# Message phase of a four-layer graph network: the offset adds go from GpSimd to VectorE, the ring of gathered rows gets seven tiles, and the one-hot of types moves to the end of VectorE's turn

## The reference, cut to what matters

```
x = layernorm(x + L0(x));  x = layernorm(x + L1(x));  ...

def L1(x):                       # 12500 edges, 16 edge types
    m_in = concat([x[src], edge_emb_W[edge_type]])
    m    = relu(m_in @ msg_W.T + msg_b)
    agg  = segment_sum(m, dst) / clip(degree, 1)
    h    = x + agg @ upd_W.T + upd_b
    return (h - mean) * rsqrt(var + 1e-5) * ln_g + ln_b
```

## Time and profile before

| | us |
|---|---|
| median of three runs | 2611.82 |
| the profiled execution's own time | 2617.21 |
| its span, first to last instruction | 2615.3 |
| DVE busy in the span | 1591.5 (61%) |
| POOL busy in the span | 1868.5 (71%) |
| PE busy in the span | 1428.1 (55%) |
| first scan (L1538) of the message phase starts | 727.97 |
| last scan starts | 1106.39 |
| first gather of the message phase starts | 702.67 |

### The profile page before, as it was taken

One profiled execution on the slowest core, in us unless ns is written; L12 is line 12 of the kernel. 1 busy time (PEld: TensorE's weight loads), 2 busy tenths in 40 slices (PEclk: granted clock), 3 DMA queues, 4 the chain that ended last, 5 costly groups with the idle time before them and its releaser, 6 DMA issues. The chain is left out here.

```text
span 2615.3 us, 21930 instructions
## 1 busy us (share of the span) xinstructions
PE 1428.1 (55%) x4580; PEld 736.3 (28%) x4580; DVE 1591.5 (61%) x4851; ACT 863.5 (33%) x1813; POOL 1868.5 (71%) x1494
## 2 busy tenths in 40 slices
PE   6787588887356665637787547445445650011111
PEld 1344244444222222213333224222222330011110
DVE  8889287777438888948777735234334565434443
ACT  0111167676326565644566612111112330000000
POOL 5773777876288887334677777777875877777787
PEclk8899699998577778769888878777777875555555
DMA  1111344433434554334454466666696883333331
GB/s 25 26 35 33 96 116 129 129 109 76 106 75 115 133 128 129 98 93 104 105 120 116 105 151 186 176 170 168 187 165 205 224 220 96 82 68 71 76 70 43
DMA packets 358129, 297.95 MB, mean 114 GB/s; under 512 B 110941, under 2 KB 312428, under 8 KB 357981
## 3 DMA queue, kind: packets, MB, share of 16 engines
q1 hardware_dynamic: 260397, 225.43, 31.5%
q0 software_dynamic: 97600, 71.11, 13.9%
HBM read 199.75 MB, written 96.70 MB: 113 GB/s over the span
## 5 line engine op out<-in xcount | busy, mean ns | idle before, releaser
L2089 PE MATMUL tl_pX<-k_ident,tl_ga 125*128 125x125 f32 x400 | 84.1, 348 | 427.9 <-DMA tl_ga<-table_TE,k_s_idxE 327.1
L2200 DVE TENSOR_TENSOR_SCAN tl_S<-tl_same,tl_S,tl_pX 128x500 f32<-128x500 bf16 x96 | 120.3, 1253 | 312.9 <-issue 181.8
L479 POOL DMA_INDIRECT tl_ga<-table_TE,k_s_idxE x200 | 242.9, 1215 | 63.4 <-issue 59.1
L2089 PEld LDWEIGHTS tl_pX<-k_ident,tl_ga 125*128 125x128 f32 x400 | 58.1, 178 | 442.4 <-DMA tl_ga<-table_TE,k_s_idxE 336.7
L479 POOL DMA_INDIRECT eq_ga<-table_T,k_idxS x100 | 124.5, 1245 | 80.8 <-ACT eq_y L1794 51.7
L479 POOL DMA_INDIRECT ms_ga<-table_T,k_idxS x100 | 134.3, 1343 | 50.8 <-issue 41.0
L479 POOL DMA_INDIRECT at_ga<-x,k_src x100 | 138.4, 1384 | 43.4 <-issue 25.2
L1269 PE MATMUL tl_pCon<-dr_BC,dn_cT 128*128 128x512 f32 x196 | 133.1, 768 | 51.8 <-ACT dn_cT L1276 25.5
L479 POOL DMA_INDIRECT tl_ga<-table_TH,k_send x100 | 123.0, 1230 | 51.2 <-issue 50.6
L281 POOL DMA_INDIRECT table_ptab<-k_ef,ix_scatI x100 | 124.9, 1249 | 46.4 <-issue 46.4
L479 POOL DMA_INDIRECT at_gb<-xw,at_dstI x100 | 129.8, 1298 | 30.5 <-issue 30.5
(11 more groups left out here) (464 smaller groups left out, 4445.9 us busy)
## 6 DMA issues: line engine op xcount, KB each, us to landing
dr_x<-x SPq DMA_DIRECT2D x97, 256.0 KB
result<-dr_o SPq DMA_DIRECT2D x97, 256.0 KB
dm_xT<-xT SPq DMA_DIRECT2D x32, 768.0 KB
tl_fac<-table_dinv SPq DMA_DIRECT2D x50, 250.0 KB
table_T<-at_y SPq DMA_DIRECT2D x50, 224.0 KB
table_T<-ms_y SPq DMA_DIRECT2D x50, 224.0 KB
table_T<-eq_y SPq DMA_DIRECT2D x50, 224.0 KB
table_TE<-tl_y SPq DMA_DIRECT2D x50, 224.0 KB
```

What stands on the lines that cost most here:

```text
L479: nc.gpsimd.indirect_dma_start(out=buf[:, k, :], out_offset=None, in_=table, in_offset=bass.IndirectOffsetOnAxis(ap=index[:, CT * c + k:CT ...
L2089: last = nc.tensor.transpose(pX[j % 2][:, k * TP:(k + 1) * TP], ga[j % RG][:, k, :], K["ident"][0:TP, 0:TP])
L2200: nc.vector.tensor_tensor_scan(S[i][:], same[j % RM][:], pX[i][:, 0:CE], 0.0 if j % NC == 0 else S[1 - i][:, CE - 1:CE], ALU.mult, ALU.add ...
```

## The change

Four edits, all in `message_phase`:

1. The two adds leave GpSimd (`biased` and the tiles `xb` are gone). VectorE does them in `second`, straight into `h2`, between `gained` and the add that was there; that add now reads `h2` and writes it in place. GpSimd's turn is eight (later four) indirect DMAs and nothing else.
2. The ring of gathered rows has seven tiles instead of five. A tile of the rings `ga` and `xt` is now free when `h2` of its chunk is made (`s_h2`), where it was free after `xb` and the first residual.
3. SyncE loads the target rows of chunk s+1 in turn s, where it loaded those of s+2.
4. `one_hot(s+3)` is the last thing in VectorE's turn, where it was second.

```
-        RG, RX, RU, RM = 5, 4, 4, 3
+        RG, RX, RU, RM = 7, 4, 4, 3
...
             def load_targets(c):
-                need(sp, s_xb, c - RX + 1)
-                need(sp, s_h1, c - RX + 1)
+                need(sp, s_h2, c - RX + 1)
                 copy_rows(sp, xt[c % RX][:], rows_of(T["T1"], CE * c, CT), s_xt[c % RX])
...
-                if live(s + 2):
-                    load_targets(s + 2)
+                if live(s + 1):
+                    load_targets(s + 1)
...
             def fetch(c):
-                need(pool, s_xb, c - RG + 1)
-                need(pool, s_h1, c - RG + 1)
+                need(pool, s_h2, c - RG + 1)
                 need(pool, s_tA, c - RG + 1)
                 need(pool, s_idx, c - PQ + 1)
...
-            def biased(c):
-                i = c % RU
-                have(pool, c)
-                pool.wait_ge(s_xt[c % RX], 32 * (c // RX + 1))
-                need(pool, s_h2, c - RU + 1)
-                nc.gpsimd.tensor_tensor(xb[i][:, 0:CT, :], xt[c % RX][:], bc(lb, CT), ALU.add)
-                nc.gpsimd.tensor_tensor(xb[i][:, CT:2 * CT, :], ga[c % RG][:], bc(lb, CT), ALU.add).then_inc(s_xb, 1)
...
             def second(c):
+                need(dve, s_y, c - 1)
+                nc.vector.tensor_tensor(h2[c % 2][:, 0:CT, :], xt[c % RX][:], bc(lb, CT), ALU.add)
+                nc.vector.tensor_tensor(h2[c % 2][:, CT:2 * CT, :], ga[c % RG][:], bc(lb, CT), ALU.add).then_inc(s_off, 1)
                 dve.wait_ge(s_hg, c + 1)
-                dve.wait_ge(s_xb, c + 1)
-                need(dve, s_y, c - 1)
-                nc.vector.tensor_tensor(h2[c % 2][:], hg[:], xb[c % RU][:], ALU.add).then_inc(s_h2, 1)
+                dve.wait_ge(s_off, c + 1)
+                nc.vector.tensor_tensor(h2[c % 2][:], hg[:], h2[c % 2][:], ALU.add).then_inc(s_h2, 1)
...
                 if live(s):
                     running(s)
-                if live(s + 3):
-                    one_hot(s + 3)
...
                     scale(s - 1, mv1, sd1, rs1, nb1, s_sd1, s_rs1, s_r1, s_n1)
+                if live(s + 3):
+                    one_hot(s + 3)
```

More of the change, by code:

```diff
@@ L1302, in message_phase @@
         ga, xt = [a.sb(f"ga{i}", [TP, CT, D]) for i in range(RG)], [a.sb(f"xt{i}", [TP, CT, D]) for i in range(RX)]
-        xu, xb = ([a.sb(f"{n}{i}", [TP, 2 * CT, D]) for i in range(RU)] for n in ("xu", "xb"))
+        xu = [a.sb(f"xu{i}", [TP, 2 * CT, D]) for i in range(RU)]
         m, oF = (a.sb(n, [D, CE]) for n in ("m", "oF"))
@@ L1318, in message_phase @@
         (s_w, s_eps, s_kind, s_tw, s_tA, s_xs, s_oneh, s_psM, s_m, s_S, s_psO,
-         s_oF, s_psR, s_mean, s_xb, s_h1, s_d1, s_d2, s_mv1, s_mv2, s_sd1, s_sd2, s_rs1, s_rs2, s_r1, s_r2, s_n1, s_hg, s_h2, s_y, s_twc, s_zero) = (
+         s_oF, s_psR, s_mean, s_h1, s_d1, s_d2, s_mv1, s_mv2, s_sd1, s_sd2, s_rs1, s_rs2, s_r1, s_r2, s_n1, s_hg, s_h2, s_y, s_twc, s_zero) = (
             a.sem(n) for n in ("weights", "eps", "kind", "typeW",
-                               "tA", "xs", "onehot", "psM", "m", "S", "psO", "oF", "psR", "mean", "xb", "h1", "stats1", "stats2",
+                               "tA", "xs", "onehot", "psM", "m", "S", "psO", "oF", "psR", "mean", "h1", "stats1", "stats2",
                                "mv1", "mv2", "sd1", "sd2", "rs1", "rs2", "scale1", "scale2", "n1", "hg", "h2", "y", "typeW_copied", "zeroed"))
+        s_off = a.sem("offset")
         s_ga, s_xt = [a.sem(f"ga{i}") for i in range(RG)], [a.sem(f"xt{i}") for i in range(RX)]
@@ L1403, in _ @@
                     last_edges(s + 3 + PQ)
-                if live(s):
-                    biased(s)
         @block.tensor
```

## The result

| | before | after |
|---|---|---|
| median of four runs each, on one chip (us) | 2612.61 | 2574.97 |
| range of the runs | 2608.99 to 2615.42 | 2566.58 to 2575.73 |
| ratio to before, 95% interval | | 0.9849 [0.9825, 0.9873] |
| profiled execution, its span | 2617.21, 2615.3 | 2575.73, 2573.9 |

The change makes the kernel 1.5% faster: -37.6 us by the medians, -41.5 in the profiled executions, against -43.6 forecast.

The account below looks back on a forecast made before the run. The prediction took GpSimd's queue of indirect DMAs to bound scans 0 to 18. Its terms, -46.1 there, 0 for scans 18 to 24 and +2.5 for the tail, total -43.6 us, giving 2568 us, range 2546 to 2593.

Parts of the forecast that it names:

- GpSimd's queue bounds 19 turns: Message phase, first 19 turns: GpSimd's queue of eight indirect DMAs a turn never rests and sets the turn.
- GpSimd's turn of 14.1 us: GpSimd without adds: 13.7 us left, plus 0.4 as DMA stretching grows from 1.6 to 2.0 in proportion to VectorE's two-input time.
- The 18 turns at that pace: Scans 0 to 18: 18 x 14.1 = 253.8 us against 299.9, a gain of 46.1.
- VectorE's turn of 12.85 us: VectorE's own load a turn with the two new adds (1.25): 12.85 us, below GpSimd's 14.1.
- The stalls go with the adds: VectorE no longer stands still beside GpSimd's adds; scans 18 to 24: +7.5 for adds, about -8 for stalls, booked 0.
- The one-hot: Moving it to the end of VectorE's turn costs nothing, since GpSimd's 14.1 us covers the old loop of 12.0.
- Seven tiles: Ring of gathered rows: fetching chunk s+3 needs h2 of chunk s-4, more than a turn of slack, nothing gained or lost.
- The tail: Stretch after the last scan: the last two `second` are on the path, +2.5 us.
- A: Rival, chance 0.13: VectorE alone bounds and GpSimd's DMAs are not stretched, 12.85 us a turn, 2546 us.
- B: Rival, chance 0.28: loops through TensorE, ScalarE and SyncE keep the turn near 15 us, 2588 us.
- C: Rival, chance 0.04: GpSimd cannot write descriptors during VectorE's 6.4 us of two-input work, turn 18.5 us, 2647 us.
- D: Rival, chance 0.05: the one-hot's wait only moves to the turn's end, turn stays 16 to 16.7 us, 2613 us.

Follow-up runs that it names:

- e4: Changed kernel with two more indirect DMAs (lookups into a spare tile) in each of GpSimd's first 19 turns: 2635.24 us, ratio 1.0079 to the kernel before.
- e8: Changed kernel with 20 lookups (five chunks) moved from GpSimd's first five turns to the end of the attention phase: 2542.82 us, ratio 0.9725 to before.
- e5: Changed kernel with all 76 lookups of last edges done in the index phase, not between the gathers: 2629.1 us, one run, read for the turns only.
- e7: Changed kernel with two idle adds of the old form (constants into spare tiles) put on GpSimd in each turn: 2632.93 us, ratio 1.0081 to before.
- e6: Changed kernel without the two adds (result lacks the offset), second sum made in two halves: 2557.45 us, ratio 0.9784 to before.
- e1: Changed kernel with the one-hot back in second place of VectorE's turn: 2584.03 us, ratio 0.9891 to before.
- e2: Kernel before with only the one-hot moved to the end of VectorE's turn: 2603.66 us, ratio 0.9961 to before.
- e3: Changed kernel with five tiles of gathered rows instead of seven: 2713.23 us, ratio 1.0387 to before.

## Why the prediction was right

*GpSimd's queue bounds 19 turns: right.* e4 lengthens it by 3.2 us and the turn by 3.3; e8 takes DMAs out of it and gains what they had cost.

*GpSimd's turn of 14.1 us: right in size, its reason not borne out.* Over the same kind of stretch as the earlier trace rows, in mid-phase, it measured 14.02. With 8 x (1.21 + 0.30) = 12.1 undisturbed, 1.9 is stretching, where 2.0 was forecast and 1.6 was there before (the DMAs of the steady stretch take 1.448 us in the mean, in the kernel before 1.405). By the Trainium skill's "SBUF — State Buffer", section "SBUF: two separate sides", the new adds would stretch nothing, and the turn would be 13.7. The trace doesn't agree: the seven DMAs that begin within the first add take 1.44 to 1.62 us. But "in proportion" is not how it comes about either. Of the 26.7 us of stretching in these 14 turns only 2.3 belong to DMAs that begin in the two adds; 7.0 belong to the second sum, and 16.0 to the 14 that begin in the scan or in the one-hot, which now stands right in front of it. What counts is which instruction an issue happens to begin in (below). That the proportion gave the right sum was luck.

*The 18 turns at that pace: nearly.* They took 255.9 us against 253.8. The forecast has no term for the filling of the pipeline: the first three turns took 47.7 us, not 42.3, and the later ones a little less than 14.1 each.

*VectorE's turn of 12.85 us: right.* Where the queue doesn't hold it, it is 12.93 in e5 (scans 1 to 18) and 12.97 in e8 (1 to 14); the late turns of after are 12.65.

*The stalls go with the adds: right.* After has none, e7 brings them back. Booked at 0 for the late turns, the balance was -2.6 us; e7 puts the stalls there at 1.7 us a turn, e6 the adds at 0.55.

*The one-hot: the step failed.* "I cost the move itself at nothing, since GpSimd's 14.1 covers the old loop of 12.0" was wrong: e1 and e2 both measure 9 us. The old loop is not 12.0 us once there are waits in it: in e1 the scans are 14.50 apart in the steady stretch, while the queue would allow 13.86, and the late turns, which GpSimd doesn't cover, are 13.38 against 12.65. Of the -37.6 us about 9 are the one-hot by the medians and, by difference, about 28 the adds with their ring.

*Seven tiles: right in number, wrong in reason.* "More than a turn of slack" holds for seven and for six. I had not seen that with five, the tile's later release would close a loop of one turn, 138 us dearer. The ring is no free extra beside the move of the adds, but its condition.

*The tail: +2.5 forecast, +3.8 measured.* The forecast counts the last two `second`; three start behind scan 24 (their first adds at 1063.73, 1073.85 and 1083.57 us), and 3 x 1.25 is 3.75. The last `gained` still waits for ScalarE, with the adds behind it, as the earlier trace rows had it:

```profile
1082.42 1.22 DVE L1553 TENSOR_TENSOR ms_hg<-ms_n,ms_lg 125x1024 f32<-125x1024 f32 x1 [2.77 <-ACT ms_n L1471]
1083.57 0.68 DVE L1557 TENSOR_TENSOR ms_h<-ms_xt,ms_lb 125x512 f32<-125x512 f32 x1
```

The sum by stretches: -44.0 (forecast -46.1), -2.6 (0), +3.8 (+2.5) make -42.8 against -43.6. The profiled executions differ by 41.5: scan 0 came 3.3 us earlier and the part behind the phase took about 5 us more, in code that was not changed.

*The rivals.* A (VectorE alone bounds) would have been right had GpSimd a lead: e8 is that kernel for its first 14 turns. B (other loops near 15) falls with e5 and e8: the same loops run at 12.9 to 13.0. C (GpSimd shut out) and D fall with the mean of 1.42 us a DMA and the turn of 14.22.

## What to carry to other kernels

Look for the queue whose idle time is all "issue": it sets the pace, and work is best taken out of it or moved to a stretch where the same queue waits for something else, as e8 does for 32 us more. Compare the paces of two engines over the same turns, and leave the filling of the pipeline out: with it in, after's queue and scans seemed 0.6 us apart, and two experiments went to a gap that wasn't there. A buffer that is freed later needs a ring long enough that free, refill, landing and use span two turns; draw that loop before believing in slack. Put an instruction that waits for another engine's result behind all work of the turn that doesn't need it, even where another engine seems to cover the wait.

## What the runs showed of the hardware

The hold between GpSimd's adds and VectorE needs no shared data: in e7, whose idle adds read constants and the row `lb`, the tiny multiply L1584, which uses neither, takes up to 2.80 us instead of 0.17. In the other direction a DMA issue is held where it begins within an instruction of VectorE with two inputs in SBUF (after, 875 to 880 us):

```profile
875.66 1.26 POOL L479 DMA_INDIRECT ms_ga<-table_T,k_idxS  x1 [0.30 <-issue]
875.75 0.68 DVE L1557 TENSOR_TENSOR ms_h<-ms_xt,ms_lb 125x512 f32<-125x512 f32 x1
...
877.14 1.23 DVE L1561 TENSOR_TENSOR ms_h<-ms_hg,ms_h 125x1024 f32<-125x1024 f32 x1
877.22 2.23 POOL L479 DMA_INDIRECT ms_ga<-table_T,k_idxS  x1 [0.30 <-issue]
```

The gather begun at 875.66 begins in the last 0.17 us of the gained rows, has the first add from 875.75 on beside it, and takes 1.26 us; the one begun 0.08 us into the second sum takes 2.23. The 112 issues of the steady stretch of after follow one pattern. Begun beside statistics, aggregation or an idle VectorE, they take 1.21 to 1.22 us. Begun within the second sum, one of the two adds, the first residual's add or the gained rows, they end 1.08 to 1.09 us behind the end of that instruction, and never take less than 1.21: 1.63 where 0.55 us of it was left, 2.23 where 1.15 was left, 1.27 where 0.18 was left. So short instructions cost little and long ones much. Begun up to 0.75 us ahead of the gained rows, they are not held (1.21). The scan is an exception:

```profile
841.80 0.47 DVE L1512 TENSOR_SCALAR ms_oneh<-ms_typ,ms_kindf 16x500 f32<-16x500 int32 x1
842.07 2.39 POOL L1387 DMA_INDIRECT k_pq<-table_ptab,k_src  x1 [0.31 <-issue]
842.19 1.24 DVE L1527 TENSOR_TENSOR_SCAN ms_S<-dst_same,ms_S,ms_m 128x500 f32<-128x500 bf16 x1
```

The issue begins 0.12 us ahead of the scan and is held through it; all 12 that begin in the one-hot, 0.06 us behind to 0.29 us ahead of the scan's start, take 2.21 to 2.55. In the kernel before, where small operations follow the one-hot, those that begin in it take 1.21 to 1.22. Why the scan holds an issue that began ahead of it is open.

A gather of four small DMAs was usable 6.1 us after the end of its last issue in after (880.96 to 887.04) and 5.8 in e3 (876.82 to 882.65); in a loop of buffers that is as long as issuing them.
